# Four rounding passes over x move from VectorE to GpSimd in the FP4 stage

## The reference

```python
def fp4_quant_dequant(x):
    xb = x.reshape(shape[:-1] + (shape[-1] // BLOCK, BLOCK))
    scale = jnp.maximum(jnp.max(jnp.abs(xb), axis=-1, keepdims=True) / 6.0, 1e-12)
    xn = xb / scale
    idx = jnp.searchsorted(_MID, jnp.abs(xn))
    return (_GRID[idx] * jnp.sign(xn) * scale).reshape(shape)
gate = fp4_linear(x, w_gate)
y = fp4_linear(x, w_up)
h = jax.nn.silu(gate) * y
return fp4_linear(h, w_down)
x = x + jnp.tanh(g_ffn[3]) * _L3_ffn_ref(_layernorm(x), w_gate, w_up, w_down)
```

## Time and profile before

| what | value |
|---|---|
| median of 3 runs | 1403.06 us (1402.62 to 1405.44) |
| the profiled execution | 1411.71 us |
| its span | 1409.9 us |
| PE busy | 1312.7 us, 93% |
| DVE busy | 1105.6 us, 78% |
| ACT busy | 694.4 us, 49% |
| POOL busy | 414.9 us, 29% |

### The profile page before, as it was taken

The page is one execution under the profiler, slowest core; times in us unless marked ns, Lnnn a source line. Parts: engine busy times, 40 slices in busy tenths (PEclk is TensorE's granted clock), DMA queues, the critical chain, the costliest instruction groups (busy, mean ns, idle before and its releaser), DMA issues. The chain is left out here.

```text
span 1409.9 us, 36465 instructions
## 1 busy us (share of the span) xinstructions
PE 1312.7 (93%) x11864; PEld 977.7 (69%) x11864; DVE 1105.6 (78%) x3711; ACT 694.4 (49%) x1639; POOL 414.9 (29%) x580
## 2 busy tenths in 40 slices
PE   5999999899899999999899889999988998998998
PEld 3777878645457777776545568878877887885666
DVE  7788778678779988889678777676764885668997
ACT  2666767544345555555434356766753323442321
POOL 1333346434433444447134423432420000000000
PEclk8999999989989999999899999999999998999999
DMA  5544455231233333334011233333346351550000
GB/s 159 157 122 125 125 151 156 83 113 49 83 100 98 85 85 95 91 85 136 14 55 49 77 106 107 87 94 103 87 131 195 133 171 43 148 144 22 16 15 23
DMA packets 134073, 138.11 MB, mean 98 GB/s; under 512 B 38601, under 2 KB 121292, under 8 KB 133836
## 3 DMA queue, kind: packets, MB, share of 16 engines
q1 hardware_dynamic: 133948, 136.51, 33.6%
HBM read 100.98 MB, written 35.48 MB: 97 GB/s over the span
## 5 line engine op out<-in xcount | busy, mean ns | idle before, releaser
L1143 DVE TENSOR_REDUCE negm<-ps 112x1 f32<-112x375 f32 x512 | 260.7, 542 | 105.1 <-PE ps L1267 102.6
L1267 PE MATMUL ps<-kst,qst 96*112 96x375 f16 x768 | 232.5, 337 | 14.4 <-DVE negm L1143 7.1
L853 ACT ACTIVATE p<-ps 125x448 f32<-125x448 f32 x336 | 177.3, 543 | 110.2 <-PE ps L1295 71.9
L1282 PE MATMUL ps<-qst,kst 112*125 112x224 f16 (+1 forms) x1152 | 210.4, 265 | 8.0 <-POOL qst L822 4.3
L822 POOL TENSOR_TENSOR qst<-m_row,diag 16x448 f16<-16x448 f16 x128 | 130.3, 1046 | 280.1 <-ACT m_row L932 275.1
L1282 PEld LDWEIGHTS ps<-qst,kst 112*125 112x125 f16 (+1 forms) x1152 | 147.0, 138 | 43.1 <-issue 9.7
L1773 PE MATMUL ps<-fw,xs_e 128*128 128x512 f16 x672 | 162.7, 386 | 0.0
L1127 DVE TENSOR_SCALAR ps<-ps 125x448 f32<-125x448 f32 x192 | 120.0, 629 | 31.2 <-PE ps L1282 31.1
L1139 DVE CUSTOM_DVE_ANT_0 with_mask<-ps,mask_add 112x375 f16<-112x375 f32 x256 | 134.3, 545 | 11.5 <-issue 10.1
L1267 PEld LDWEIGHTS ps<-kst,qst 96*112 96x112 f16 x768 | 96.9, 131 | 47.5 <-DVE negm L1143 21.2
L1190 PE MATMUL ps<-wkv_split,ctxT 128*125 128x256 f16 x864 | 121.0, 277 | 0.4 <-DVE ks L1098 0.4
(11 more groups left out here) (262 smaller groups left out, 2512.3 us busy)
## 6 DMA issues: line engine op xcount, KB each, us to landing
k_split<-ks SPq DMA_DIRECT2D x48, 375.0 KB, 3.6
kst<-k_split SPq DMA_DIRECT2D x96, 187.5 KB, 2.9
fw<-in_w SPq DMA_DIRECT2D x16, 1024.0 KB, 7.2
qst<-q_split SPq DMA_DIRECT2D x96, 112.0 KB, 2.4
kst<-k_split SPq DMA_DIRECT2D x96, 93.8 KB, 2.6
stage<-in_ctxT SPq DMA_DIRECT2D x16, 375.0 KB, 4.0
ctxn<-in_ctx SPq DMA_DIRECT2D x16, 375.0 KB
rows<-x SPq DMA_DIRECT2D x48, 112.9 KB, 2.8
```

Source lines behind the costliest of these rows:

```text
L853: act.activation(p[p_of[hg]][kt], ps[0:KR, BK_ST + n % 2, 0:4 * S], ACT.Exp).then_inc(s_exp, 1)
L1143: dve.tensor_reduce(g.negm[1 - par][:, h:h + 1], scored, AX_X, ALU.max, negate=True).then_inc(s_max, 1)
L1267: mm = pe.matmul(ps[0:S, BK_S + h % 2, 0:SK], g.q_stack[q][0:96, h, :], g.k_stack[q][0:96, h // 2, :], start=True, stop=True)
L1282: mm = pe.matmul(bank[:, 2 * r * S:2 * (r + 1) * S], g.k_stack[par][0:rows, pr, kt * KR:(kt + 1) * KR], g.q_stack[par][0:rows, 2 * pr:2 * ...
```

## The change

For the 256 columns of x, four of the rounding passes go to POOL: scaling, `onto_grid`, `off_grid` and `scale_back`. [...] DVE does these passes for the 704 columns of h alone; `largest`, `block_scale`, `inverse_scale` and `grid_step` stay in one go over 960 columns. So in a turn POOL waits for DVE's inverse scales, scales x and raises `s_xscaled`, for which DVE's `grid_step` waits; `grid_step` raises `s_grid`, behind which POOL runs `carry`, the maximum, add, subtract and multiplication and raises `s_qx`. PE's x transposes wait for `s_qx`, its h transposes for `s_q`; DVE's next `block_scale` waits for `s_qx` as well, since it overwrites the scales.

```diff
@@ scalar
-                at_least(act, s_scaled, b)
+                at_least(act, s_xscaled, b - 1)
                 act.activation(raw[:, 0:D], rows_of.x[:, b, :], ACT.Identity, ...).then_inc(s_xn, 1)
+                act.wait_ge(s_xn, b + 1)
+                act.activation(x_negated[:, :], raw[:, 0:D], ACT.Copy, scale=-NUDGE).then_inc(s_xneg, 1)
@@ gpsimd
+                t = Rounding(x_negated[:, :], rounded[par][:, 0:D], *room)
+                pool.wait_ge(s_inv, i + 2)
+                pool.wait_ge(s_xneg, i + 2)
+                pool.tensor_tensor(t.scaled, t.src, t.wide(t.amax), ALU.mult).then_inc(s_xscaled, 1)
+                pool.wait_ge(s_grid, i + 2)
+                carry(pool, g)
+                step(pool.tensor_scalar(t.magic, t.magic, MAGIC, None, ALU.max))
+                step.sync()
+                step(pool.tensor_tensor(t.scaled, t.magic, t.scaled, ALU.add))
+                step.sync()
+                step(pool.tensor_tensor(t.scaled, t.magic, t.scaled, ALU.subtract))
+                step.sync()
+                at_least(pool, s_t, i + 1)
+                pool.tensor_tensor(t.dst, t.scaled, t.wide(t.scale), ALU.mult).then_inc(s_qx, 1)
+            skewed(step, 2 * 3, -1, NT - 3, pairs, body, start=3)
@@ vector
-                    t = Rounding(raw[:, cols], rounded[par][:, cols], *room)
+                    t = Rounding(raw[:, cols], rounded[par][:, cols], *(room if rows else hidden_room))
+                    h = Rounding(raw[:, D:WIDTH], rounded[par][:, D:WIDTH], *hidden_room)
                     step(largest(dve, t))
                     step.sync()
+                    dve.wait_ge(s_qx, min(i + 2, NT) if isinstance(i, int) else i + 2)
+                    if hidden:
+                        at_least(dve, s_q, i)
                     step(block_scale(dve, t))
                     step.sync()
-                    step(inverse_scale(dve, t))
-                    step.sync()
-                    scale_negated(dve, t).then_inc(s_scaled, 1)
-                    dve.wait_ge(s_scaled, i + 3)
-                    step(grid_step(dve, t))
+                    inverse_scale(dve, t).then_inc(s_inv, 1)
+                    if hidden:
+                        dve.wait_ge(s_inv, i + 2)
+                        scale_negated(dve, h).then_inc(s_scaled, 1)
+                        dve.wait_ge(s_scaled, i + 1)
+                    if rows:
+                        dve.wait_ge(s_xscaled, i + 2)
+                    grid_step(dve, t).then_inc(s_grid, 1)
+                if hidden:
+                    dve.wait_ge(s_grid, i + 2)
+                    step(onto_grid(dve, h))
                     step.sync()
-                    step(onto_grid(dve, t))
+                    step(off_grid(dve, h))
                     step.sync()
-                    step(off_grid(dve, t))
-                    step.sync()
-                    if rows:
-                        at_least(dve, s_t, i + 1)
                     if not isinstance(i, int) or i >= 2:
                         dve.wait_ge(s_ht, i - 1)
-                    scale_back(dve, t).then_inc(s_q, 1)
+                    scale_back(dve, h).then_inc(s_q, 1)
@@ tensor
-                    pe.wait_ge(s_q, i + 2)
+                    pe.wait_ge(s_qx, i + 2)
-                    pe.wait_ge(s_q, i + 2)
+                    pe.wait_ge(s_q, i)
```

More of the change, by code:

```diff
@@ L2454, in fp4_ffn @@
         "x_turned", "xT", "gate_up", "silu", "h_turned", "hT"))
-    s_y, s_x, s_dve = (sem(n) for n in ("y", "x", "dve"))
+    s_y, s_x, s_dve, s_pool = (sem(n) for n in ("y", "x", "dve", "pool"))
+    s_inv, s_xneg, s_xscaled, s_grid, s_qx = (sem(n) for n in (
+        "inverse_scales", "x_negated", "x_scaled", "grid_steps", "x_rounded"))
     gate = g.gates[:, 7:8]
@@ L2463, in fp4_ffn @@
     xqT = sb("xqT", [128, KC, ROWS], F32)
+    x_negated = sb("x_negated", [ROWS, D], F32)
+    hidden_room = tuple(t[:, first:] for t, first in zip(room, (D // QB, D // QB, D, D)))
     silu = sb("silu", [ROWS, N3], F32)
@@ L2516, in _, with body @@
             skewed(Steps(act, s_dve), 0, -2, NT, pairs, body, start=3)
+        @block.gpsimd
+        def _(pool):
+            step = Steps(pool, s_pool)
+            def body(turn):
+                i, par = turn.i, turn.u
+                t = Rounding(x_negated[:, :], rounded[par][:, 0:D], *room)
[13 more added lines that the diff above has]
+            skewed(step, 2 * 3, -1, NT - 3, pairs, body, start=3)
         @block.vector
@@ L2520, in _ @@
             step = Steps(dve, s_dve)
-            for n, s in enumerate((s_xn, s_scaled, s_q)):
+            for n, s in enumerate((s_xn, s_qx)):
                 dve.memset(g.scratch_dve[0:1, 4 + n:5 + n], 0.0).then_inc(s, 1)
@@ L2532, in body @@
                     dve.wait_ge(s_silu, i + 1)
-                    at_least(dve, s_scaled, i + 2)
+                    at_least(dve, s_scaled, i)
                     dve.tensor_tensor(raw[:, D:WIDTH], silu[:, :], gate_up[1], ALU.mult).then_inc(s_hm, 1)
@@ L2541, in body @@
                         dve.wait_ge(s_hm, i + 1)
-                    at_least(dve, s_q, i + 2)
                     step(largest(dve, t))
                     step.sync()
+                    dve.wait_ge(s_qx, min(i + 2, NT) if isinstance(i, int) else i + 2)
+                    if hidden:
+                        at_least(dve, s_q, i)
                     step(block_scale(dve, t))
                     step.sync()
-                    step(inverse_scale(dve, t))
+                    inverse_scale(dve, t).then_inc(s_inv, 1)
[9 more added lines that the diff above has]
+                    step(onto_grid(dve, h))
                     step.sync()
-                    scale_negated(dve, t).then_inc(s_scaled, 1)
-                    dve.wait_ge(s_scaled, i + 3)
-                    step(grid_step(dve, t))
+                    step(off_grid(dve, h))
                     step.sync()
-                    step(onto_grid(dve, t))
-                    step.sync()
-                    step(off_grid(dve, t))
-                    step.sync()
-                    if rows:
-                        at_least(dve, s_t, i + 1)
                     if not isinstance(i, int) or i >= 2:
                         dve.wait_ge(s_ht, i - 1)
-                    scale_back(dve, t).then_inc(s_q, 1)
+                    scale_back(dve, h).then_inc(s_q, 1)
                 if isinstance(i, int) and i == -1:
@@ L2573, in body @@
                                              scalar=gate, in1=rows_of.x[:, i - 2, :], op0=ALU.mult, op1=ALU.add).then_inc(s_x, 1)
-            skewed(step, 2 * 6, -1, NT + 1, pairs, body, start=3)
+            skewed(step, 2 * 4, -1, NT + 1, pairs, body, start=3)
             step.sync()
```

## The result

| | before | after |
|---|---|---|
| median | 1403.06 us (1402.01 to 1406.33, 5 runs) | 1411.97 us (1409.45 to 1414.09, 5 runs) |
| ratio of after to before, 95% interval | | 1.0043 [1.0026, 1.0060] |
| the profiled execution, its span | 1411.71, 1409.9 us | 1409.45, 1407.5 us |

Slower by 0.43%, which is 6 us (3.6 to 8.4); the plain medians stand 8.9 us apart, but the ratio with its interval is what is used here. That is over the 0.2% bound, on the side that had a chance of 0.40. The forecast was +1.9 us. By the ratio the time is 1409.1 us: inside the stated 1399 to 1410.5, outside the forecast's own 1402 to 1407.

A forecast was written before the change was run, and what follows sets the result against it. DVE and PE were both taken as full, with DVE releasing PE. Waits of 1.08 us against 1.06 saved gave +0.24 over twelve bodies, plus 0.8 and 0.85: +1.9, so 1405.0 us, range 1399 to 1410.5 (forecast's own 1402 to 1407).

The forecast's parts named there:

- the side that had a chance of 0.40: Whole kernel: slower by more than 0.2% (2.8 us), from the dear cases (0.30) and the forecast's upper end.
- grid step waits for POOL's scaling: Full body: DVE's grid step starts at 1.56 instead of 0.93, behind POOL's scaling of x, +0.63 us.
- waits on register values: Eight loop bodies: three such waits where there was one, about 0.1 us each body, +0.8 us.
- last body: Stage's end: x leaves POOL late, gate/up starts 1.1 us later, less 0.27 of slack: +0.85 us.
- POOL's price: Rival, chance 0.25: maximum costs 0.73 (+3.7 us) or broadcast read 1.05 (+3.8): about 1408.8, both 1412.5.
- ACT's copy costs nothing: Between normed_row and silu: ScalarE's added copy, 0.6 us a body (0.48 to 0.66), is covered by its waits.
- The rival of the whole turn: Rival, chance 0.05: turns last the whole instruction, waits sum to 1.89, net +0.83 us a body, about 1414.7.
- the PE-bound one: Rival, chance 0.17: POOL and DVE don't collide or DVE keeps ahead, PE sets the pace, about 1398 us.
- `carry` slips in ahead: Around onto_grid: carry, priced 0.187 us, gets in ahead; the maximum follows at 2.98 and delays off_grid by 0.07.
- the prediction's own rule of turns: POOL and DVE passes over two SBUF tensors take turns, all but 0.15 us; passes with PSUM input run beside POOL.
- a period near 8.8 to 8.9: Sign in the changed profile: a body's period near 8.8 to 8.9 us, where it was 8.77.
- Over two SBUF tensors: Condition for turns: DVE passes reading two SBUF tensors collide with POOL, among them four of the five 704-column passes.

The follow-up runs named there:

- The two runs with a product: Changed kernel with POOL's maximum replaced by a two-input multiplication by ones, with and without the carry: 1.0040 and 1.0048 of before.
- beside memsets: Changed kernel with POOL's five passes made memsets of about their length and the carry dropped: 1403.83 us against 1404.36, 0.9993 of before.
- the kernel with POOL present: Kernel before plus five dependent 1x1 multiplications on POOL in each turn, of no use: 1404.71 us against 1406.7, 0.9985.
- the repetition: Changed kernel run again, unchanged, against before: 1410.22 us against 1404.36, 1.0045 [1.0033, 1.0058].
- before against itself: Kernel before run again, unchanged, as the null: 1405.99 us against 1406.7, 1.0001 [0.9988, 1.0014].
- the kernel with the early update: Kernel before with the update's add on POOL, fed by an ACT copy ahead of the turned x's copy: 0.9967 of before, then 0.9994.

## Why the prediction came out as it did

Per body in the loop, from the timeline above and the one of before; the grid step's and `block_scale`'s terms less the 0.04 that each start took before:

| term | predicted, us | measured, us |
|---|---|---|
| four narrower passes | -1.06 | -1.06 |
| grid step waits for POOL's scaling | +0.63 | +0.54 to 0.65 |
| `off_grid` held by the maximum | +0.07 | +0.23 |
| `scale_back` held by the add | +0.38 | +0.32 to 0.41 |
| waits on register values (start of `block_scale`) | +0.10 | +0.15 |
| a loop body | +0.12 | +0.3 (9.08 for 8.77, 8.98 for 8.69) |
| last body | +0.85 | +0.70 |
| all bodies (first to last `h` product) | +1.9 | +4.0 |

The mechanism was right in the main and its size too small, +1.9 us where the stage shows +4.0. That the time still falls in the stated range is partly luck: the range reached so far up for another reason, POOL's price. Right: that POOL and DVE take turns, all but the last 0.15 us, and that the wins are given back by it; the grid step's wait, named as the largest, with POOL's scaling "held about 0.5" (1.33 for 0.62, so 0.71); `scale_back`'s hold, to 0.06; that ACT's copy costs nothing (0.42 beside its long waits, under the 0.48 that was its lower bound); and the late gate/up at the end. The grid step's term is right as a sum of two sizes that were off: the broadcast multiplication takes 0.62 and not 0.73, the hand-over from POOL to DVE 0.10 to 0.21 and not 0.07. The rival of the whole turn is refuted (its waits were 0.78, 0.40 and 0.71), the PE-bound one was never reached. The rival of POOL's price came true in its condition, a maximum of 0.73 or more, and not in its mechanism: `off_grid` was to wait 0.31 more and waited 0.16 more. That its 1408.8 is near the measured 1409.1 is luck.

Wrong: "`carry` slips in ahead, POOL's maximum gets in at 2.98 and frees DVE at 3.22". The carry comes 0.05 behind `onto_grid`, not ahead of it, and takes 0.89 for its 0.18. It was costed at its free length, which no row beside a busy DVE warranted: the earlier trace rows had shown that a POOL pass over 128x256 waits, and DVE's own step to `onto_grid` is 0.03. So the maximum came in 0.16 later than said, head-on with `off_grid`. Its length was mis-sized too: 0.83, above the 0.73 that was given as the bound. By the prediction's own rule of turns 0.83 would from there hold `off_grid` 0.63 (less the 0.02 of its lead and the 0.18 that its sums take off), and the 0.42 that was taken 0.22. It holds 0.23: as a hold 0.42 was right, as a length it wasn't. So the step of the carry is what made 0.23 of 0.07. That is worked out: without the carry the maximum would come in 0.14 ahead of `onto_grid`'s end, at 1337.60, keep DVE out for 0.24 as it does now, and hold `off_grid` (1337.78) by about 0.07. The two runs with a product show the same step by itself (0.55 with the carry, 0.41 without). In after it is +0.16 a body, 1.9 us for twelve: most of what was missing.

The waits on register values were 0.05 too small (0.4 us over eight bodies), and their reason was misread. The prediction had 8.77 for a body in the loop and 8.69 for one outside, but in before 8.77 and 8.69 alternate within the loop, and the 0.08 lies ahead of `scale_back` (0.12 for 0.04). What is new in after is 0.19 for 0.04 ahead of `block_scale`, in the eight loop bodies alone. It is there beside memsets too, so it is no turn; that it comes from register values was not tested. One body of 9.34 had a grid step wait of 0.95, where DVE started 0.47 behind POOL's end and not 0.1 to 0.2; that is in both profiles of after, and not explained. The sign "a period near 8.8 to 8.9" failed with these terms: it is 8.98 and 9.08.

One reading of the rows was too narrow. The DVE instruction of 0.40 in the earlier trace rows is a tensor_scalar that reads one SBUF tensor, and it held POOL. So did the grid step, of the same kind, in the kernel with POOL present. "Over two SBUF tensors" is thus not the whole condition. It changed nothing in the sum, as POOL has no pass beside the grid step in after.

Open: the runs give +6 us (3.6 to 8.4, and 4.6 to 8.1 in the repetition), the stage 4.0 (second profiles) to 4.9 (first ones, with the body at the lower clock). The 4.0 lies within the first interval and just under the second. POOL present without work and before against itself show nothing outside the stage, but before's own two profiles differ by 4.4 us ahead of it. In other kernels too the time and the stretch differ by some us: -1 against -4.4 with memsets, +5.6 against +7.1 with the product.

## What to carry to other kernels

Work that is taken off a full engine is no gain if both engines then read SBUF through the same door: price each pair of overlapping instructions by how long one keeps the other out, and put POOL's reads beside what has an input in PSUM or is a reduction. A tiny POOL instruction in such a chain waits out a whole pass of the other engine (0.89 for 0.18) and uses up the lead that the next POOL pass would have had, which was 0.14 us a body in the runs with a product. And a wait of the fast engine for the slow one in mid-chain (here the grid step) can cost more than the holds: with that pass left on DVE the change is even (1.0007).

## What the runs showed of the hardware that was not expected

- A one-input POOL pass over 128x256 f32 with a constant (tensor_scalar, maximum) takes 0.83 us, longer than the two-input one (0.72), but holds a DVE pass of two SBUF tensors 0.23 against 0.55. Why is not shown.
- A two-input POOL pass whose second tensor is read 16 times over takes 0.62, less than the plain one (0.73).
- A DVE tensor_scalar over 128x60 (`block_scale`), free at 0.19, took 0.38 beside POOL's add in the kernel with the early update, and the grid step (tensor_scalar, 128x960) made POOL's 1x1 multiplication take 0.66 for 0.18. So one SBUF input is not enough to be free of turns, while the reduction `largest` kept its 1.15 beside the same add:

```profile
1332.19 0.38 DVE L2389 TENSOR_SCALAR room_xh<-room_xh 128x60 f32<-128x60 f32 x1
```
